# The fourth layer's masks on ScalarE, its closing work inside its sweep, and the first sweep's transposes two units ahead

## The reference

```
x = layernorm(x + L0(x, adj))     # signed attention, 3 heads, and two GRU cells
x = layernorm(x + L1(x, adj))     # normalised adjacency product
x = layernorm(x + L2(x, adj))     # attention, 2 heads
x = layernorm(x + L3(x, adj))

def L3(x, adj):                   # 4 heads of 64 features
    h = (x @ W).reshape(n, 4, 64)
    s_src, s_dst = einsum(h, a_src), einsum(h, a_dst)
    e = leaky_relu(s_src[:, None] + s_dst[None], 0.2)
    e = where((adj > 0.5)[:, :, None], e, -1e9)
    alpha = softmax(e, axis=0)
    return einsum('ijh,ihc->jhc', alpha, h).reshape(n, 256) + bias
```

## Time and profile before

| | us |
|---|---|
| median of 3 runs | 2473.22 (2455.23 to 2474.8) |
| the profiled execution | 2473.49 |
| its span, first to last instruction | 2471.8 |
| mean granted TensorE clock | 0.92 of 2.4 GHz |
| busy: PE, DVE, ACT, POOL | 2136.4, 1606.7, 727.5, 249.5 |

### The profile page before, as it was taken

One profiled execution on the slowest core, in us unless ns is written; L12 is line 12 of the kernel. 1 busy time (PEld: TensorE's weight loads), 2 busy tenths in 40 slices (PEclk: granted clock), 3 DMA queues, 4 the chain that ended last, 5 costly groups with the idle time before them and its releaser, 6 DMA issues. The chain is left out here.

```text
span 2471.8 us, 25679 instructions
## 1 busy us (share of the span) xinstructions
PE 2136.4 (86%) x9784; PEld 1167.7 (47%) x9784; DVE 1606.7 (65%) x2540; ACT 727.5 (29%) x1013; POOL 249.5 (10%) x130
## 2 busy tenths in 40 slices
PE   6999999669999999996999489977999466999990
PEld 5555565324444444464555144445999441222340
DVE  2454443767768687642777833343888648999887
ACT  2222211668788788752222100001000110000000
POOL 0000000000000000000000000000000006656540
PEclk9999978779999999998999799997999777999995
DMA  5555534354554454453000045431000105323211
GB/s 167 188 187 181 192 125 166 139 183 169 178 187 170 170 194 158 128 164 118 1 0 1 0 129 137 132 80 46 10 17 10 58 1 183 88 88 92 67 51 45
DMA packets 132867, 271.86 MB, mean 110 GB/s; under 512 B 14822, under 2 KB 45384, under 8 KB 128880
## 3 DMA queue, kind: packets, MB, share of 16 engines
q1 hardware_dynamic: 114416, 240.84, 30.8%
q10 hardware_dynamic: 18324, 29.34, 3.2%
HBM read 226.76 MB, written 43.37 MB: 109 GB/s over the span
## 5 line engine op out<-in xcount | busy, mean ns | idle before, releaser
L854 PE MATMUL banks<-arena 128*128 128x512 f32 (+1 forms) x1512 | 584.6, 546 | 35.5 <-DVE arena L1463 29.0
L854 PEld LDWEIGHTS banks<-arena 128*128 128x128 f32 x1512 | 268.3, 191 | 349.5 <-issue 340.2
L1687 DVE SCALAR_TENSOR_TENSOR arena<-arena 128x1024 f32<-128x1024 f32 (+3 forms) x264 | 324.1, 1301 | 24.8 <-PE banks L986 14.1
L1463 DVE TENSOR_TENSOR arena<-arena 128x1536 f32<-128x1536 f32 (+2 forms) x132 | 201.6, 1527 | 149.9 <-ACT arena L1130 121.6
L772 PE MATMUL banks<-arena 128*128 128x512 f32 (+2 forms) x528 | 251.7, 607 | 0.0
L915 PE MATMUL banks<-arena 128*128 128x512 f32 (+2 forms) x528 | 209.3, 548 | 46.1 <-DVE arena L1562 45.0
L977 PE MATMUL banks<-arena 128*64 128x512 f32 (+3 forms) x1056 | 223.9, 563 | 12.8 <-DVE arena L1687 12.8
L952 PE MATMUL banks<-arena 128*124 128x129 f32 (+2 forms) x1936 | 218.4, 275 | 13.8 <-DVE arena L1644 13.8
L952 PEld LDWEIGHTS banks<-arena 128*124 128x124 f32 (+2 forms) x1936 | 216.7, 187 | 15.7 <-issue 12.8
L669 POOL TENSOR_SCALAR arena<-arena 128x1024 bf16<-128x1024 f32 (+1 forms) x66 | 208.2, 3157 | 133.2 <-DVE arena L1687 125.4
L1398 DVE CUSTOM_DVE_ANT_0 arena<-arena 128x2708 f32<-128x2708 bf16 (+1 forms) x66 | 196.3, 2974 | 4.1 <-DVE arena L1392 4.1
(11 more groups left out here) (189 smaller groups left out, 2039.5 us busy)
## 6 DMA issues: line engine op xcount, KB each, us to landing
arena<-adj_T SPq DMA_DIRECT2D x210, 256.0 KB, 3.0
arena<-hw_rows SPq DMA_DIRECT2D x126, 384.0 KB, 3.2
arena<-in_adj SPq DMA_DIRECT2D x21, 1354.0 KB
adj_T<-arena ACTq DMA_DIRECT2D x105, 256.0 KB, 2.1
arena<-in_adj SPq DMA_DIRECT2D x25, 1024.0 KB
arena<-in_adj SPq DMA_DIRECT2D x42, 512.0 KB
hw_rows<-arena SPq DMA_DIRECT2D x21, 384.0 KB, 2.6
arena<-in_adj SPq DMA_DIRECT2D x21, 330.0 KB
```

Source lines behind the costliest of these rows:

```text
L854: ins = PE.matmul(bank(2 * (c % 2) + f)[:, 0:wid(c)], hs[0:R, m % 3, h * D + f * P:h * D + (f + 1) * P], E[0:R, n % 3, h, 0:wid(c)], start ...
L1463: V.tensor_tensor(e, e, a, ALU.mult).then_inc(s["p_ok"], 1)
L1687: V.scalar_tensor_tensor(PM3[0:k, n % 2, h, 0:w], r3_bc[0:k, h, c * WW:c * WW + w], smalls[0:k, 4, h * T + t:h * T + t + 1], mask3[0:k, n ...
```

## The change

First sweep: TensorE's order becomes transposes of unit n + 2, products of unit n.

Fourth layer: the masks move from GpSimd to ScalarE, as two passes with Relu: the first makes a steep ramp out of the strip that is 0 above 0.5 and at least 1 below, the second turns it around. `PM3` has three buffers. `rawT3` holds one chunk. The closing work is done in pairs of tiles: eight pairs (two chunks of four pairs) inside the sweep, at units t = 3, 7, 11, 15 of the following chunk for TensorE and two, four and six units later for the other steps; the last three pairs after it. GpSimd adds the mean for targets without an edge, ScalarE scales by the inverse divisors, VectorE does the divisors, the sum, the statistics and the normalising. Each pair has a store of its own. The barriers after the sweep go. Some semaphores are shared (`projs[0]` for `u_xt_ps` and `u_xt_ok`), with counts that start at T.

```diff
+STEEP = float(2 ** 24)
+DT = WW // P
-        rawT3 = sb(RAW3, N)
+        rawT3 = sb(RAW3, WW)
-        PM3 = sb(2, H3, WW)
+        PM3 = sb(3, H3, WW)
+        def pair_at(n, first):
+            c, t = divmod(n, T)
+            if c and t >= first and (t - first) % 4 == 0 and (t - first) // 4 < DT // 2:
+                return (c - 1) * DT // 2 + (t - first) // 4
+            return None
+        LAST = range((CW - 1) * DT // 2, T // 2)
...
# sync engine
             for n in range(UNITS3):
                 strip3(sp, n)
-            stage_end(sp, "sp")
-            stage_end(sp, "sp")
-            (two stores of the whole output)
+                if kept < LAST[0] and n == T * (1 + kept // (DT // 2)) + 15 + 4 * (kept % (DT // 2)):
+                    store(kept)          # waits for fin_norm, one or two transfers
+                    kept += 1
+            for v in range(kept, T // 2):
+                store(v)
...
# GpSimd
-                G.tensor_scalar(mask3[...], strips3[...], 0.5, None, ALU.is_gt).then_inc(l3_mask, 1)
+            for v in range(T // 2):
+                pool.wait_ge(fin_zz, v + 1)
+                for nr, ts in pair_parts(v):
+                    for g in range(ts.start, ts.stop):
+                        link(G.tensor_tensor(zt3[...], z, sum_bc[...], ALU.mult))
+                        link(G.tensor_tensor(xnat[0:nr, g, :], xnat[0:nr, g, :], zt3[0:nr], ALU.add))
+                pool.sem_inc(fin_zero, 1)
...
# TensorE
             transposes_A(0)
+            transposes_A(1)
             for n in range(UNITS):
-                if n + 1 < UNITS:
-                    transposes_A(n + 1)
+                if n + 2 < UNITS:
+                    transposes_A(n + 2)
                 products_A(n)
...
+            def backs(v):
+                if v:
+                    pe.wait_ge(fin_scaled, v)
+                for i, g in enumerate((2 * v, 2 * v + 1)):
+                    for k in range(RAW3):
+                        ins = PE.transpose(bank(6 + i)[0:kp(g), k * P:(k + 1) * P], rawT3[:, k, ...], ident)
+                ins.then_inc(back_ps, 1)
...             (in the sweep, after a unit's products)
+                v = pair_at(n, 3)
+                if v is not None:
+                    pe.wait_ge(l3_read, RAW3 * c)
+                    backs(v)
+            pe.wait_ge(l3_read, RAW3 * CW)
+            for v in LAST:
+                backs(v)
...
# ScalarE
+            def above(n):
+                act.wait_ge(l3_in[n % 3], 16 * (n // 3 + 1))
+                S.activation(strip, strip, ACT.Relu, bias=edge3[...], scale=-STEEP).then_inc(l3_above, 1)
+            def masked(n):
+                act.wait_ge(l3_above, n + 1)
+                if n >= 3:
+                    act.wait_ge(l3_p, H3 * (n - 2))
+                S.activation(mask3[...], strips3[...], ACT.Relu, bias=ones[...], scale=-1.0).then_inc(l3_mask, 1)
+            def scaled(v):
+                act.wait_ge(fin_dd, v + 1)
+                if v:
+                    act.wait_ge(fin_var, v)
+                (per tile and head: S.activation(t3[64 columns], bank(6 + i)[...], ACT.Copy, scale=dd3[...]))
+                ins.then_inc(fin_scaled, 1)
+            def rooted(v):
+                act.wait_ge(fin_var, v + 1)
+                S.activation(r, r, ACT.Sqrt).then_inc(fin_std, 1)
+            above(0)
+            for n in range(UNITS3):
+                if n + 1 < UNITS3:
+                    above(n + 1)
+                masked(n)
+                if c and t == 2:
+                    chunk_out(c - 1)
+                if pair_at(n, 7) is not None:
+                    scaled(pair_at(n, 7))
+                if pair_at(n, 9) is not None:
+                    rooted(pair_at(n, 9))
+            chunk_out(CW - 1)
+            scaled(LAST[0])
+            for v in LAST:
+                if v + 1 in LAST:
+                    scaled(v + 1)
+                rooted(v)
...
# VectorE, after a unit's four products (divisors: 2 copies, is_equal, add, reciprocal;
# added: sum, 2 bn_stats, 2 bn_aggr, add EPS; normed: reciprocal, 2 tensor_scalar)
+                if pair_at(n, 5) is not None:
+                    divisors(pair_at(n, 5))      # waits for back_ps
+                if pair_at(n, 9) is not None:
+                    normed(pair_at(n, 9))        # waits for fin_std
+                if pair_at(n, 7) is not None:
+                    added(pair_at(n, 7))         # waits for fin_scaled and fin_zero
+            divisors(LAST[0])
+            for v in LAST:
+                added(v)
+                if v + 1 in LAST:
+                    divisors(v + 1)
+                normed(v)
```

More of the change, by code:

```diff
@@ L346, in build @@
         stored = sem("stored")
-        back_ps, back_ok = sem("back_ps"), sem("back_ok")
+        l3_edge, l3_above, back_ps = sem("l3_edge"), sem("l3_above"), sem("back_ps")
+        fin_zz, fin_dd, fin_zero, fin_scaled, fin_var, fin_std, fin_norm = (
+            sem(f"fin_{s}") for s in ("zz", "dd", "zero", "scaled", "var", "std", "norm"))
         h2_out, h2_back = sem("h2_out"), sem("h2_back")
@@ new lines, in scaled @@
+            def scaled(v):
+                act.wait_ge(fin_dd, v + 1)
+                if v:
+                    act.wait_ge(fin_var, v)
+                for i, g in enumerate((2 * v, 2 * v + 1)):
+                    nr = kp(g)
+                    for h in range(H3):
+                        ins = S.activation(t3[0:nr, i, h * C3:(h + 1) * C3], bank(6 + i)[0:nr, h * C3:(h + 1) * C3], ACT.Copy,
+                                           scale=dd3[0:nr, g, h:h + 1])
+                ins.then_inc(fin_scaled, 1)
@@ L1679, in _, with divisors, added, normed @@
             dve.wait_ge(rest_bc["r3"], 16)
+            def divisors(v):
+                dve.wait_ge(back_ps, v + 1)
+                d, z = dd3[:, 2 * v:2 * v + 2, :], zz3[:, 2 * v:2 * v + 2, :]
+                for i, g in enumerate((2 * v, 2 * v + 1)):
+                    nr = kp(g)
+                    ins = V.tensor_copy(dd3[0:nr, g, :].unsqueeze(2),
+                                        bank(6 + i)[0:nr, D:D + P].rearrange("p (h c) -> p h c", h=H3)[:, :, 0:1])
+                link(ins)
+                V.tensor_scalar(z, d, 0.0, 1.0 / N, ALU.is_equal, ALU.mult).then_inc(fin_zz, 1)
+                dve.wait_ge(fin_zz, v + 1)
+                link(V.tensor_tensor(d, d, z, ALU.add))
+                V.reciprocal(d, d).then_inc(fin_dd, 1)
+            def added(v):
+                dve.wait_ge(fin_scaled, v + 1)
+                dve.wait_ge(fin_zero, v + 1)
+                for nr, ts in pair_parts(v):
+                    x = xnat[0:nr, ts, :]
+                    ins = V.tensor_tensor(x, x, t3[0:nr, ts.start - 2 * v:ts.stop - 2 * v, :], ALU.add)
+                link(ins)
+                for g in (2 * v, 2 * v + 1):
+                    ins = stats(g)
+                link(ins)
+                for g in (2 * v, 2 * v + 1):
+                    ins = V.bn_aggr(mv[0:kp(g), g, :], bnst[0:kp(g), g, :])
+                link(ins)
+                for nr, ts in pair_parts(v):
+                    ins = V.tensor_scalar(rstd[0:nr, ts], mv[0:nr, ts, 1], EPS, None, ALU.add)
+                ins.then_inc(fin_var, 1)
+            def normed(v):
+                dve.wait_ge(fin_std, v + 1)
+                r = rstd[:, 2 * v:2 * v + 2]
+                link(V.reciprocal(r, r))
+                for g in (2 * v, 2 * v + 1):
+                    x = xnat[0:kp(g), g, :]
+                    ins = V.tensor_scalar(x, x, mv[0:kp(g), g, 0:1], rstd[0:kp(g), g:g + 1], ALU.subtract, ALU.mult)
+                ins.then_inc(fin_norm, 1)
+            V.memset(dd3, 1.0)
             for n in range(UNITS3):
```

142 lines of the change are left out of this document (58 added, 84 removed).

## The result

The changed kernel took 2441.22 us (median of 4 runs, 2439.18 to 2446.49) against 2473.58 of the kernel before (4 runs, 2455.23 to 2474.8): ratio 0.9885, 95% interval 0.9842 to 0.9928. That is 1.3% less by the medians and 0.7 to 1.6% by the interval. 2450, which is 0.9% less, had been forecast. The profiled execution took 2442.71 with a span of 2441.0, 30.8 us less than before.

The account below looks back on a forecast made before the run. TensorE was taken to bound both sweeps, VectorE right behind it in the fourth layer's and alone in the tail. -41.3 + 3.6 + 7 - 1.4 + 0.5 + 8 = -23.6 from 2473.5 gave 2450, -0.9%, range 2433 to 2467.

Parts of the forecast that it names:

- The tail: After the fourth layer's sweep: only pairs 8 to 10 are left, 68.8 us become 27.5; -41.3, bounds -36 and -45.
- the 24 to 33 that was to be its sign: Stretch after the fourth layer's last product: should be 24 to 33 us; more breaks the tail's term.
- The sweep's payment: Fourth layer's sweep: eight pairs closed inside cost +3.6 (to +7) in the middle chunk, +7 (3.6 to 14) in the last.
- VectorE's surplus of 6 us: Middle chunk, units 5 to 21: VectorE 102 us against TensorE's 96; the third product buffer hides the 6.
- 4.0 to 4.2: Fourth layer's last chunk: a sign, TensorE's starts between units 5 and 21 should spread to 4.0 to 4.2 us.
- GpSimd's weight on VectorE: Fourth layer's sweep: GpSimd's 3.4 us per pair beside VectorE's products stretch them by 1.0 us per pair.
- Rival (2): Sweep: GpSimd's small operations block VectorE for their whole length, 3.4 instead of 1.0 us a pair; +13, 2463; chance 0.14.
- The masks: Fourth layer: masks on ScalarE are hidden, VectorE drops to 4.87 us, TensorE stays at 5.44; -1.4, and +0.5 at the start.
- Transposes two ahead: First sweep: longer waits for data at chunk starts, +6.2, plus half of 3.8 for the clock; +8 (0 to +14).
- The half of 3.8 for the clock: First sweep's chunk starts: the new wait may lower the clock two units earlier, 3.8 us more, half of it counted.
- (1): Rival: cover holds everywhere, pair work hidden in the last chunk too, first sweep's loads early enough; -39, 2434; chance 0.17.
- (3): Rival: ScalarE's wait for divisors holds back masks, TensorE stops at eight pairs, 6.4 us each; 2501, +1.1%; chance 0.09.

Follow-up runs that it names:

- e5_tail_apart: Changed kernel with two product buffers and all eleven pairs closed after the sweep, none inside: 2472.24 us, ratio 1.0012 to the kernel before.
- e4_ring2: Changed kernel with two product buffers instead of three: 2445.84 us, ratio 0.9903 to the kernel before.
- e3_pool_masks: Changed kernel with its masks made by GpSimd again, the mean's additions between them: 2457.1 us, ratio 0.9954 to the kernel before.
- e9_best_one: Changed kernel with transposes one unit ahead, early row sums, and the last three pairs in banks and buffers of their own: 2406.63 us, ratio 0.9737.
- e10_best_two: Changed kernel, transposes still two units ahead, with early row sums and the last three pairs in banks and buffers of their own: 2389.3 us, ratio 0.9693.
- e1_one_ahead: Changed kernel with the first sweep's transposes one unit ahead again: 2435.03 us, ratio 0.9847 to the kernel before.
- e8_tail_banks: Changed kernel with the last three pairs in PSUM banks and scaled buffers of their own: 2438.14 us, ratio 0.9877 to the kernel before.

## Why the prediction held

**The tail** (-41.3 forecast, bounds to -45): -45.2. The mechanism was right and the small terms too dear. From the last product to the third addition's end took 20.0 us, root and normalising 1.2, the store 2.3, 23.5 together with all gaps included, where the sum had 25.4 and 2.1 more for handovers: these were in the steps already. It lies just under the 24 to 33 that was to be its sign. The rest is the pair's cycle, 5.5 instead of 6.1 twice (scaling eight heads 1.75 instead of 2.0), and the first pair, where GpSimd's four operations took 2.74 instead of 3.4 (2421.60 to 2424.34): a row of 128 columns is not half of one of 256, which took 0.61 to 0.64. No table load joined at a root.

**The sweep's payment** (+3.6 and +7, less 1.4 for the masks): +2.0 and +8.1 measured, -1.6 in the first chunk; +8.5 against +9.2 together. That they agree so well is in part luck: e5_tail_apart, which has the masks' move and no pair in the sweep, puts the masks at -3.7 over the three chunks (forecast -1.4, for the first two) and so the pairs at +12.2 (forecast +10.6). TensorE's six transposes, 0.9 in the sum, took 0.80. That the third product buffer hides VectorE's surplus of 6 us in the middle chunk was tested: without it the middle chunk is 5.8 us longer. VectorE was to be the bound in the last chunk alone, and it is. What I had wrong is the picture: the starts don't spread to 4.0 to 4.2 from unit 5 on. VectorE's lead holds the pace at 3.62 until it is used up, and the waits come in the last 40% of the chunk, 1.7 us the first time. Products took 1.30 us (1.27 forecast), and TensorE's starts in the first chunk are 5.44 apart, as forecast. The prediction called itself wrong if TensorE's waits in the sweep pass 15 us: they are 15.9, but 11.5 of them are the wait for the first product, which was 12.8 before, and 4.4 are new.

**GpSimd's weight on VectorE** (1.0 us per pair): e5_tail_apart has none of it in the sweep, and its products take 1.280 and 0.901 us instead of 1.301 and 0.941. 168 x 0.021 + 84 x 0.040 = 6.9 us, 0.86 per pair. The number of buffers plays no part in it: e4_ring2, with two and the pairs inside, has 1.299 and 0.941. Rival (2) had asked for 3.4.

**The masks**: -1.4 forecast, and the first chunk is 1.6 us shorter. But it is as short with the masks on GpSimd and three buffers (125.6) and with two buffers and the masks on ScalarE (125.4), so either of the two takes that away. The prediction costed the masks as an edit of their own; their worth stood in the row above it, in the 4.87 us of a unit's products, and e3_pool_masks puts 16 us on it. At the sweep's start +0.5 was forecast and -1.2 measured; e3_pool_masks gives 1.5 of it back.

**Transposes two ahead** (+8, of it 6.2 by arithmetic): +5.1 in the profile, 5 to 7 in the tests. The waits themselves grew by more than the 6.2, by 8.6: 5.0 at the four full starts and 1.5 at the fifth, as worked out, and 2.0 inside chunks, which stood only in the upper bound. The reason given, the products of another unit queued behind the waiting transposes, is borne out by the wait of 3.70 instead of 2.39 and by the sums of waits, 9.9 and 18.5 us. The half of 3.8 for the clock had the wrong sign at the first start: after the longer wait the clock was back sooner (0.97 of full speed from 100 to 160, where the kernel before had 0.91), and so 8.6 us more waiting cost 5. What I didn't see, and what was in the earlier trace rows, is that the row sum's place could be moved: 25 us lay there in the kernel before's order, and 30 in the changed one.

**The rivals.** (1), all covered, has its tail (-45) but not its sweep. (3), stops at the pair points, did not occur: the longest wait inside the last chunk was 1.43 us, and the clock of the two chunks with pairs is 0.98 and 0.96. Since ScalarE's waits for the divisors never emptied the ring of masks, nothing was queued long enough to stop TensorE.

The sum came out 7 us too high (profiled: -30.8 against -23.6): 3.9 from the tail, 2.9 from the first sweep, 0.7 from the fourth and 1.7 from its start, less the 2.1 of scatter in the stages between. The mechanisms of the two large terms held. But the likeliest single outcome had been a change under 1% (0.49, against 0.42 for a larger gain), and the measured 1.3% is past that line by the medians, with the line inside its interval.

## What to carry to other kernels

Work that follows a loop is cheap only beside an engine with room: make the room first (here the masks off the neighbour that slowed VectorE), then a deeper ring between the two engines, then put the work in. Alone, the masks' move was worth about 5 us and the closing in pairs nothing. When an in-order engine waits for data, more lookahead puts more ready work behind the wait; look instead for whoever holds the buffer, and where its release stands in that engine's order. Where runs of one kernel fall in two groups, compare profiled spans group by group before believing a median.

## What the runs showed of the hardware

**Two clock levels for the same work.** In e9_best_one and e10_best_two TensorE entered the narrow chunk (products of 148 columns) full, with 5.00 of 5 us busy, and was granted 1.00 of 2.4 GHz in one execution and 0.50, the 1.2 GHz level, in the other. It cost 20 us. The kernel before shows 0.50 there in its one profile, and 9 of its 47 executions were 16 to 20 us shorter than its median; so were 1 of 4 of e1_one_ahead and 8 of 18 of the four kernels with early row sums. That those are the same event is likely by its size, and by the mean granted clock of each execution: 0.928 to 0.931 in the short ones of the kernel before, 0.917 to 0.921 in its others, and likewise 0.940 to 0.945 against 0.930 to 0.932 with early row sums. But only one short execution has a profile, and why the clock falls in one execution and not in the next stays open. One thing goes with the order of the work: of the 44 executions of the six kernels with two units of lead and late row sums, the changed one among them, none was short. In the changed kernel TensorE waits 1.71 us right before the narrow chunk, in the kernel before 0.20. So the second unit of lead probably costs the short executions too, which the 5 to 7 us from profiles of long ones don't hold.

**GpSimd held by a short VectorE addition.** In e8_tail_banks one operation of 128 x 256 on GpSimd took 0.62 us alone and 1.14 when it started beside VectorE's addition of two operands in SBUF:

```profile
2422.51 0.62 POOL L704 TENSOR_TENSOR arena<-arena 128x256 f32<-128x256 f32 x1
...
2424.02 1.14 POOL L704 TENSOR_TENSOR arena<-arena 128x256 f32<-128x256 f32 x1 [0.18 <-POOL arena L706]
```

VectorE's 0.69 (it started 0.02 earlier) is unchanged from 0.68 in the changed kernel, so GpSimd alone paid 0.52 of it. The Trainium skill ("SBUF — State Buffer", section "Who interferes with whom") says that a VectorE instruction with two SBUF inputs contends with a GpSimd instruction that reads SBUF, and that this is an exclusive lock. In this pair the trace nearly agrees: 0.52 of 0.69. In e8_tail_banks' other such pair, at 2420.58, it took 1.14 as well. In the sweep the loss is split: the windows of the changed kernel give GpSimd 15.21 + 13.12 = 28.3 us for 32 such operations, which are 20 at 0.62, so it lost 8.3, and VectorE lost the 6.9 of above.
